# A two-layer graph kernel: the closing products taken in fours of groups, and one-hot factors built by scalar comparisons with a third of their products on ScalarE

## The reference, cut to what matters

```
h = relu(layernorm(x))
x = x + MLP([h, segment_sum(relu([h[src], edge_attr] @ W1 + b1) @ W2 + b2, dst)])
h = relu(layernorm(x))
x = x + segment_sum(h[src] * edge_weight[:, None], dst)
```

## Time and profile before

| what | value |
|---|---|
| median of 3 runs | 2448.67 us |
| the profiled execution: its own time / its span | 2431.01 us / 2429.2 us |
| mean granted TensorE clock | 0.901 of full speed |
| PE busy, DVE busy, ACT busy, POOL busy | 1904.6, 1580.8, 951.0, 1703.7 us |
| first phase, start of the gathers to the end of the last | about 65.6 to 2213.8 us |
| second phase, first product to the end of the span | about 2236.8 to 2429.2 us |

### The profile page before, as it was taken

How to read it: one execution, slowest core, us unless ns; L and a number is a source line. 1 busy time by engine, 2 the same in 40 slices (tenths; PEclk the granted TensorE clock), 3 DMA queues, 4 the chain that set the end, 5 groups by cost and what they waited for, 6 DMA issues and landing times.

```text
span 2429.2 us, 54571 instructions
## 1 busy us (share of the span) xinstructions
PE 1904.6 (78%) x19815; PEld 1568.8 (65%) x19815; DVE 1580.8 (65%) x4958; ACT 951.0 (39%) x2318; POOL 1703.7 (70%) x1663
## 2 busy tenths in 40 slices
PE   5766577667867787778778878888887988898898
PEld 5545455555655665667667767767776877777776
DVE  6856567666766666666666766667766766765443
ACT  3334344344444434434444444444444444442111
POOL 7777777777777777777777777777777777773000
PEclk9988888888888898889889989999999999998999
DMA  3345546544854684478358738857774775665897
GB/s 91 116 149 172 172 152 208 187 162 142 258 181 131 201 271 144 125 223 274 118 179 241 231 103 236 236 156 208 218 211 120 217 210 150 176 193 151 260 292 223
DMA packets 533582, 454.81 MB, mean 187 GB/s; under 512 B 296946, under 2 KB 485346, under 8 KB 527168
## 3 DMA queue, kind: packets, MB, share of 16 engines
q1 hardware_dynamic: 480516, 395.61, 52.1%
q0 software_dynamic: 52064, 53.17, 8.9%
q10 hardware_dynamic: 732, 2.48, 0.4%
HBM read 278.99 MB, written 172.09 MB: 186 GB/s over the span
## 4 chain that ended last, share of the span: by engine, by line
POOL 67%; issue 20%; PE 6%; DMA 4%; DVE 1%; SPq 0%; ACT 0%; POOLq 0%; ACTq 0%
POOL rows L729 67%; DMA stage<-adjacency 3%; PE pair L1162 2%; PE pair L974 1%; DMA x_all<-in_x_dram 1%; PE pair L1169 1%; PE pair L1176 1%; PE pair L1077 0%; PE pair L962 0%; PE pair L1063 0%; SPq L592 0%; DVE mean L1271 0%; PE pair L1184 0%; PE pair L1092 0%; DMA rows<-table,idx 0%
## 5 line engine op out<-in xcount | busy, mean ns | idle before, releaser
L729 POOL DMA_INDIRECT rows<-table,idx x1616 | 1656.1, 1025 | 509.1 <-issue 492.2
L842 ACT COPY stage<-pair 128x300 f32<-128x300 f32 x1616 | 622.9, 414 | 700.5 <-PE pair L1063 696.7
L1063 PE MATMUL pair<-bld 128*128 128x300 bf16 x4848 | 811.2, 325 | 4.7 <-DVE bld L1482 4.5
L1063 PEld LDWEIGHTS pair<-bld 128*128 128x128 bf16 x4848 | 568.0, 122 | 194.4 <-issue 32.2
L1035 PE MATMUL pair<-w1b,rings 128*128 128x128 f32 x1616 | 294.6, 339 | 456.2 <-DVE rings L1452 456.0
L1035 PEld LDWEIGHTS pair<-w1b,rings 128*128 128x128 f32 x1616 | 253.3, 238 | 504.6 <-DVE rings L1452 503.7
L1452 DVE TENSOR_TENSOR rings<-rows,pair 128x512 f32<-128x512 f32 x202 | 138.6, 686 | 524.2 <-DMA rows<-table,idx 523.4
L1482 DVE TENSOR_TENSOR bld<-bld,part 128x512 bf16<-128x512 bf16 x1212 | 432.6, 409 | 0.0
L1478 DVE TENSOR_SCALAR bld<-iota_key,key 128x300 bf16<-128x300 f16 x1616 | 387.0, 301 | 0.0
L834 ACT ACTIVATE rings<-rings 128x512 f32<-128x512 f32 x202 | 127.9, 633 | 364.5 <-DVE rings L1452 364.3
L1476 DVE TENSOR_TENSOR bld<-iota_lo,lo 128x512 bf16<-128x512 f16 x404 | 170.2, 421 | 139.9 <-PE pair L1063 135.3
(11 more groups left out here) (157 smaller groups left out, 1080.6 us busy)
## 6 DMA issues: line engine op xcount, KB each, us to landing
late_piece<-adjacency SPq DMA_DIRECT2D x207, 480.0 KB
rings<-in_edge_attr_dram SPq DMA_DIRECT2D x202, 256.0 KB
stage<-adjacency SPq DMA_DIRECT2D x72, 480.0 KB, 5.0
adjacency<-stage SPq DMA_DIRECT2D x28, 1200.0 KB
rows<-table,idx POOLq DMA_INDIRECT x1616
adjacency<-stage SPq DMA_DIRECT2D x20, 1080.0 KB
adjacency<-stage SPq DMA_DIRECT2D x20, 960.0 KB
adjacency<-stage SPq DMA_DIRECT2D x20, 840.0 KB
```

The source lines that it names most:

```text
L729: pool.indirect_dma_start(out=rows[:, slot, t, :], out_offset=None, in_=table, in_offset=bass.IndirectOffsetOnAxis(ap=idx[:, g, t:t + 1], ...
L842: act.copy(tiles[:, g % STAGE, :, t * WT:(t + 1) * WT], build_bank[i % 3][:, 0:KEYS].rearrange("p (h w) -> p h w", w=WT)).then_inc(tile_ke ...
L1063: last = pe.matmul(build_bank[i % 3][:, 0:KEYS], hot_w[q % 2][k][:, :, u], hot_key[q % 2][:, u, :], start=(k == 0), stop=(k == PARTS - 1))
```

## The change

Four edits.

1. **Second phase by quads.** The loop runs over 51 steps (50 of four groups, one of two) in place of 101 batches. One matmul takes 192 columns (four groups) of one block in place of 96. A piece is one chunk of four groups; there are 87 pieces in place of 101. The buffers for partial sums (SLOTS = 4), for the sums in PSUM, for the turned sums and for the placing one-hots are doubled in width or number, so SLOTS = 4 now lets loads run four quads ahead. The one-hot for placing is 112 columns wide (WB) in place of 144.
2. **The last chunk lies side by side.** Each group's store is split in two: the body, and the last chunk, which goes to a new DRAM tensor `tail` in which the last chunks of four groups are contiguous in each partition. 188 of the 202 groups still store a body. In the second phase the last chunk is read from `tail`.
3. **Comparisons.** `hot_eq` is made by four `tensor_scalar` comparisons of 128 elements, one per tile, in place of one `tensor_tensor` of 512.
4. **The third part on ScalarE.** The product of `hot_eq` with the third part of the weight is made by ScalarE, as four activations of 128 elements with a per-partition scale, in place of one VectorE `tensor_tensor` of 512 per quad. ScalarE does the two quads of the next step after `keep_eaT`, and copies the 8 scales of a group to float32 first (`far_now`). TensorE waits for `far_made` beside `quad_made`, and VectorE's next-but-one comparison waits for `far_made` before it overwrites `hot_eq`.

```diff
-WB = 144
+WB = 112
...
             def make_quad(q):
                 g, t = q // 2, q % 2 * 4
                 wait_count(dve, tile_built, 4 * (q - 1))
-                dve.tensor_tensor(hot_eq[q % 2], iota_lo[:, :, :], over(lo[:, g, t:t + 4], P), ALU.is_equal).then_inc(eq_made, 1)
+                wait_count(dve, far_made, q - 1)
+                for u in range(4):
+                    last = dve.tensor_scalar(hot_eq[q % 2][:, :, u], iota_lo[:, :], lo[:, g, t + u:t + u + 1], None,
+                                             ALU.is_equal)
+                last.then_inc(eq_made, 1)
...
-                for k in range(PARTS):
+                for k in range(PARTS - 1):
                     last = dve.tensor_tensor(hot_w[q % 2][k], hot_eq[q % 2], over(part[k][:, g, t:t + 4], P), ALU.mult)
...
+            def weigh_last(q):
+
+                g, t = q // 2, q % 2 * 4
+                if t == 0:
+                    act.copy(far_now[:, g % TWO, :], part[PARTS - 1][:, g, :]).then_inc(far_moved, 1)
+                act.wait_ge(eq_made, q + 1)
+                act.wait_ge(far_moved, g + 1)
+                wait_count(act, tile_built, 4 * (q - 1))
+                for u in range(4):
+                    last = act.activation(hot_w[q % 2][PARTS - 1][:, :, u], hot_eq[q % 2][:, :, u], ACT.Copy,
+                                          scale=far_now[:, g % TWO, t + u:t + u + 1])
+                last.then_inc(far_made, 1)
...
                         if s + 2 < GROUPS:
                             keep_eaT(s + 2, s % TWO, ea_bank)
+                        if s + 1 < GROUPS:
+                            weigh_last(2 * s + 2)
+                            weigh_last(2 * s + 3)
...
             def store_adjacency(g):
...
                 sp.wait_ge(tile_kept, (g + 1) * T)
-                sp.dma_start(adjacency[g, :, skip:ROW], stage[:, g % STAGE * ROW + skip:(g % STAGE + 1) * ROW]
-                             ).then_inc(adj_stored[g % STAGE], 16)
+                if has_body(g):
+                    sp.dma_start(adjacency[g, :, skip:last], stage[:, slot * ROW + skip:slot * ROW + last]
+                                 ).then_inc(adj_stored[slot], 16)
+                at = g % QUAD * CW
+                sp.dma_start(tail[g // QUAD, :, at:at + CW], stage[:, slot * ROW + last:(slot + 1) * ROW]
+                             ).then_inc(tail_stored[slot], 16)
...
-            def load_partial(b):
-                if b >= SLOTS:
-                    sp.wait_ge(u_kept, b - SLOTS + 1)
-                sp.dma_start(s_back[:, b % SLOTS, :], sums_of(b, 1)).then_inc(s_loaded[b % SLOTS], 16)
+            def load_partial(q):
+                wait_count(sp, u_kept, q - SLOTS + 1)
+                n = len(batches_of(q))
+                sp.dma_start(s_back[:, q % SLOTS, 0:n * COLS], sums_of(2 * q, n)).then_inc(s_loaded[q % SLOTS], 16)
...
+            def load_piece(q, n, c):
+                slot, many = n % PIECES, groups_of(q)
+                wait_count(sp, piece_used, n - PIECES + 1)
+                to = piece[:, slot, 0:many * CW]
+                if c == CHUNKS - 1:
+                    sp.dma_start(to, tail[q, :, 0:many * CW]).then_inc(piece_loaded[slot], 16)
+                else:
+                    sp.dma_start(to.rearrange("p (g w) -> p g w", g=many),
+                                 adjacency[QUAD * q:QUAD * q + many, :, c * CW:(c + 1) * CW].rearrange("g p w -> p g w")
+                                 ).then_inc(piece_loaded[slot], 16)
...
-            def multiply(b):
-                bank = u_bank[b % 2]
-                wait_count(pe, u_kept, b - 1)
...
+            def multiply(q):
+                bank, many = end_bank[q % 2], groups_of(q)
+                wait_count(pe, u_kept, q - 1)
...
+                    for h in range(BLK):
+                        k = c * BLK + h
+                        last = pe.matmul(half_of(bank, k)[:, 0:many * GC], h2[:, k * D:(k + 1) * D], held[:, :, h, :],
+                                         start=(i == 0 and h < 2), stop=(k >= NB - 2))
                     last.then_inc(piece_used, 1)
...
             def put(b):
-                pe.wait_ge(u_turn_kept, b + 1)
+                q, i = b // 2, b % 2
+                pe.wait_ge(u_turn_kept, q + 1)
                 pe.wait_ge(place_made, b + 1)
-                wait_count(pe, acc2_added, b)
+                wait_count(pe, acc2_added, b - 1)
```

More of the change, by code:

```diff
@@ L632, in fast_end @@
                 chunk = 0
-                for b in range(BATCHES):
-                    load_partial(b)
-                    for i, (low, high) in enumerate(pieces(b)):
-                        load_piece(b, FIRST_PIECE[b] + i, low, high)
-                    if b >= LAST_BATCH[chunk] + 6:
+                for q in range(ENDS):
+                    load_partial(q)
+                    for i, c in enumerate(chunks_left(q)):
+                        load_piece(q, FIRST_PIECE[q] + i, c)
+                    if q >= LAST_BATCH[chunk] // 2 + 4:
                         store_out(chunk, chunk % 2)
@@ L1156, in multiply @@
                     pe.wait_ge(piece_loaded[slot], 16 * (n // PIECES + 1))
-                    if b == 0 and high == CHUNKS:
-                        pe.wait_ge(h2_staged, CHUNKS)
-                    width = (high - low) * BLK * GC
-                    held = piece[0:NP, slot, 0:2 * width].rearrange("p (g h c) -> p g h c", g=2, c=GC)
-                    for h in range(low * BLK, high * BLK):
-                        last = pe.matmul(half_of(bank, h), h2[:, h * D:(h + 1) * D], held[:, :, h - low * BLK, :],
-                                         start=(i == 0 and h < low * BLK + 2), stop=(h >= NB - 2))
@@ L1171, in put, with turn_u @@
+                    last.then_inc(piece_used, 1)
+            def turn_u(q):
+                pe.wait_ge(u_kept, q + 1)
+                wait_count(pe, u_turn_kept, q - 1)
+                for i in range(len(batches_of(q))):
+                    last = pe.matmul(turn_bank[q % 2][:, i * D:(i + 1) * D], u_side[:, q % 2, i * P:(i + 1) * P],
+                                     twice[:, :], start=True, stop=True)
+                last.then_inc(u_turned, 1)
             def put(b):
-                pe.wait_ge(u_turn_kept, b + 1)
+                q, i = b // 2, b % 2
+                pe.wait_ge(u_turn_kept, q + 1)
```

146 lines of the change are left out of this document (79 added, 67 removed).

## The result

The changed kernel takes **2558.33 us** (median of 4 runs, 2538.43 to 2569.28) where the kernel before takes 2447.27 (median of 4, 2431.14 to 2454.11): ratio 1.046 [1.041, 1.051], slower. The forecast was 2385 us and the range ended at 2440; both its direction and its range were wrong. A kernel's executions fall into a fast and a slow state, and a ratio here compares the fast ones alone, so it can differ from the quotient of the medians beside it. The profiled execution took 2548.74 us (span 2546.9), against 2431.01 before.

A forecast was written before the change was run, and what follows sets the result against it. Gathers on POOL were taken to bound the first phase, DMA load depth the second. Gains of 44 + 20 = 64 us gave 2448.7 − 64 = 2385 us, chance 0.55; the range was 2352 to 2440.

The forecast's parts named there:

- the price of a gather begun among comparisons: First phase, POOL: 0.05 us of stretch per start among comparisons, 0.24 among products; 87 us in place of 130.6, gain 44.
- the same stretch for both: First phase: comparisons stretch gathers as products do, 0.166 us a start, 827 starts, 137 us, a loss of 6 us.
- The rule I set aside: DVE and GpSimd share ports under an exclusive lock; new comparisons hold it at least as firmly: loss of 6 us or worse.
- Rival D: First phase, POOL: strided comparisons hold every gather, 0.26 us at each of 827 starts; slower, 2513 us, chance 0.10.
- Rival B: First phase: comparisons stretch gathers as products do, POOL loses 6 us, second phase gains 20; 2435 us, chance 0.17.
- The second phase: After the gathers: loads up to 8 pieces ahead in place of 4 raise DMA share to 0.96; gain 20 us, ends 0 and 28.
- Rival C: Second phase gives nothing because DMA was near its limit already, in windows of 0.97; 2405 us, chance 0.18.
- ScalarE's part: First phase, ACT: eight activations of 0.38 us and one copy add 3.3 us a step, 8.0 of 10.4; cost zero.
- DVE's extra time: First phase: 0.12 us more per quad, 0.24 a step, hidden in 2.6 us of idle; 49 us if that cover were gone.
- The 188 more stores: SP's queue: forecast as 202 more issues, covered even at 1 us each by 1028.1 us of waiting at L540.
- PE would have passed a gain on: First phase: PE's late step takes 9.2 us against a group of 10.4 after the change, 1.2 us to spare.
- L757's mean: Sign in the first phase: mean gather time falls from 1025 ns to about 998; staying or rising means Rival B or D.

The follow-up runs named there:

- light_cmp: light_before with four comparisons of 128 elements in place of one of 512; 2642.4 us, ratio 1.084 [1.080, 1.087].
- light_before: The kernel before with most of PE's direct and late products left out; 2440.8 us, ratio 1.001 [0.998, 1.003].
- end_only: The kernel before with the second phase by quads, `tail` and WB = 112 alone; 3358.27 us, ratio 0.997 [0.992, 1.001].
- end_late: end_only with the output stores eight quads behind the last batch of their chunk in place of four; 3326.96 us, ratio 0.998 [0.994, 1.002].

## Why the prediction was wrong

**The step that failed** is the price of a gather begun among comparisons, b = 0.05 us a start, 588 × 0.05 = 29 us, and with it the rule that a gather's stretch goes by the operation it begins in. The forecast was 239 × 0.24 + 588 × 0.05 = 87 us and nothing for all other starts. By the table above, the changed kernel has 116 starts among products, 58 us; 475 among comparisons, 137 us; and 1025 elsewhere, 52 us: 246 us in all. Of the 137 us, 129 fall on the 290 starts among the old comparisons of 300 elements and 8 on the 185 among the new ones. So the low price came true for the gathers begun among the new comparisons, and failed for those that begin before a run of them and are carried into it. The forecast had no term for that.

The price was taken from one row, the gather at 2136.71 among L1478, and carried over to the new comparisons because they are "nearer in form". Over the whole trace of the kernel before, the 233 gathers begun among L1478 are stretched by 0.11 us in the mean, so even there one row was too little. The new comparisons differ in things that I did not weigh: they write every fourth element, they are short, and four stand back to back. My bad end for this term, "the same stretch for both", a loss of 6 us, was no bound either: nothing in the rows of before excluded an operation that holds more than a product does. A bound worked out from rows that lack the thing has to be the length of all that could hold the gather, one operation after another: the gather at 2038.38 in `light_cmp` was held for 1.25 us, through products and the run behind them. Two slips in the sums are small: the product that goes is a third of 1.08 us, so 0.72 us remain and not 0.74 (233 starts, 1.4 us less), and SP gets 188 more stores, not 202.

**The rule I set aside was nearer to what happened.** The lock rule of the Trainium skill (SBUF — State Buffer, section SBUF: two separate sides) says that a DVE operation in a two-port mode takes the shared ports whole and that GpSimd is blocked until it ends; on descriptors made by GpSimd the page adds that the wait lasts until DVE's end and some 115 ns. This case agrees in that distance: the gathers shown end 0.12 us behind the end of one comparison. The rule is told of one operation; here a gather stayed held across a whole run. For a comparison of 300 elements, to which the rule would seem to apply as well, the gather at 2136.71 shows no stretch. I let the exception speak for the whole class.

**Rival D** described what happened, mechanism and place: strided comparisons hold the gathers, POOL in the first phase. It decides at 0.182 us a start. With its count of 827 starts the measured stretch is 246.4 / 827 = 0.298 us (591 gathers do begin among a quad's operations, and not every one is held). It was priced at 2513 us, with 0.26 us a start and the second phase's gain; without that gain and at 0.298 its own sum gives 2448.7 + 116 = 2565 us, and 2558 were measured. Its chance of 0.10 rested on "it needs comparisons to be worse than products" as if that were unlikely. Rival B, the same stretch for both, fell by the same number.

**The second phase** (20 us forecast, 0 measured) failed on a queue that I had not followed. I read the wait for sums at L592 as the depth's price and gave 2 × SLOTS as the cure. That wait did shrink, to 26.8 us. What I left out is that `store_out` stands in SP's order behind the loads of quad LAST_BATCH // 2 + 4 and waits for a sum made at PE's step LAST_BATCH // 2 + 3. Loads run four quads ahead, so SP stands still for about three quads, the lead is used up, and it starts again from little. Before, the store stood behind the loads of batch LAST_BATCH + 6 and waited for the sum of batch step LAST_BATCH + 3, with loads four batches ahead: SP stood still for about one batch, 31.0 us in all. The change turned "what is late next" from the sums to the stores. The bound of 28 us was too low as well: with the stores at + 8 the phase falls by 36 us, with DMA at 0.97 where I took 0.96, and TensorE's granted clock at 1.00. Rival C, that DMA was at its limit already, named the right size for the wrong reason: at the same bytes the share rises from 0.76 to 0.97.

**What held.** ScalarE's part was hidden: the chain has 0% of ACT, eight products took 2.76 to 2.78 us, 0.35 each, against 0.38 estimated, and PE waited for them once in the whole span, 0.3 us. DVE's extra time was hidden, 569.6 us of waiting remain. Four comparisons take 0.96 us, 0.24 each, against 0.22 taken. The 188 more stores cost nothing that the chain shows. PE would have passed a gain on: `light_before` shows that it was not the bound. And L757's mean of 1096 ns in place of 998, named beforehand as the row that would show B or D, did.

## What stays open, and the best version

The best version that the runs point to is `end_late_act`: the second phase by quads with the stores at + 8, the third part on ScalarE, the old single comparison. It met only chips with PE's slow issue, where its ratios are 1.014 [1.009, 1.018], 1.012 [1.006, 1.017] and 1.001 [0.998, 1.005]. Where the gathers set the pace I estimate it at about 2438 − 36 − 35 = 2367 us: 36 us from the second phase, and 35 from the stretch (66 us in `end_only` and 55 in `end_late`, 22 to 31 in its three runs, so 24 to 44 less; the kernel before has 130 where the gathers set the pace, so it may be more). It is an estimate; no run shows it, and no run with the stores at + 8 met a chip where the gathers set the pace. The same holds for the new comparisons in turn with the old ones: their stretch of 40 to 48 us is below that of `end_only`, 66, but their time was seen on slow-issue chips alone (1.047 in the full kernel). Whether a run of contiguous short comparisons, or of strided long ones, would hold a gather is open too. And why PE issues at 0.70 us apart on four chips of five, and why less stretch goes with more time there, is not settled.

## What to carry to other kernels

When work is added to DVE beside gathers that POOL starts, price it by its form and by its run, and ask what a gather that begins earlier will run into: short operations that write with a stride, back to back, held a gather until the last of them had ended, while longer contiguous ones let it through between them. When loads are made to run further ahead, follow everything else in their queue: a store that waits for a result must stand behind more loads than the lead, or it eats the lead. And when one row is the only witness of a price, ask whether it shows the new operation's form or only its name.

## What was not expected of the hardware

- Four comparisons of 128 elements writing with a stride of four cost the gathers 205 us over 404 quads, 0.51 us a quad, though they replace a single operation of 512 elements with two sources (`light_cmp` against `light_before`). In turn with contiguous ones most of the stretch is gone (185 to 40 us, on a chip with PE's slow issue).
- A held gather ends 0.12 us behind the end of one comparison: 262 of the 381 gathers stretched by more than 0.1 us in `light_cmp`.
- TensorE's granted clock in the second phase was 0.86 to 0.90 while DMA came in bursts (0.72 in one window), and 1.00 when the same products were fed steadily.
- On four of five chips PE began single products 0.70 us apart over long stretches with nothing awaited, and the kernel took 3344 to 3409 us in place of 2438.
